# Writing out 39 expert slots on every engine, and a new way of numbering and adding their results

## What is computed

```
x = x + attention(layernorm(x), context)
bids = sigmoid(h @ conf_w.T + conf_b) * wealth        # h = layernorm(x), 8 experts
top_bids, selected = top_k(bids, 2)
weights = softmax(top_bids)
expert_e(h) = (silu(h @ gate_e.T) * (h @ up_e.T)) @ down_e.T     # 128 -> 512 -> 128
x = x + weights[0] * expert_first(h) + weights[1] * expert_second(h)
```

## Time and profile before

| what | us |
|---|---|
| median of 3 runs | 534.74 (534.35 to 538.36) |
| the profiled execution | 535.53 |
| its span in the trace | 533.8 |
| PE busy | 475.3 |
| DVE busy | 352.8 |
| ACT busy | 313.2 |
| POOL busy | 168.9 |

### The profile page before, as it was taken

The page is one execution under the profiler, slowest core; times in us unless marked ns, Lnnn a source line. Parts: engine busy times, 40 slices in busy tenths (PEclk is TensorE's granted clock), DMA queues, the critical chain, the costliest instruction groups (busy, mean ns, idle before and its releaser), DMA issues. The chain is left out here.

```text
span 533.8 us, 11413 instructions
## 1 busy us (share of the span) xinstructions
PE 475.3 (89%) x4013; PEld 334.3 (63%) x4014; DVE 352.8 (66%) x646; ACT 313.2 (59%) x625; POOL 168.9 (32%) x301
## 2 busy tenths in 40 slices
PE   7789999999999999999999987979987888878840
PEld 7455555555555565555555534978887887878840
DVE  7788797888887987987889823686233332323317
ACT  2248787787777877777878784302454554445500
POOL 8141412312412312324111001023555556455420
PEclk9659999999999999999999998896999999899995
DMA  7503143243342343331222000800211111111126
GB/s 191 140 21 91 46 101 100 76 114 99 91 124 78 89 119 85 80 91 47 61 56 62 18 1 6 233 1 5 41 37 41 34 39 39 34 39 34 34 74 183
DMA packets 32257, 38.14 MB, mean 71 GB/s; under 512 B 5604, under 2 KB 20580, under 8 KB 32212
## 3 DMA queue, kind: packets, MB, share of 16 engines
q1 hardware_dynamic: 27252, 30.79, 21.5%
q0 software_dynamic: 2560, 5.25, 3.8%
q10 hardware_dynamic: 2400, 1.51, 1.0%
HBM read 16.58 MB, written 4.72 MB: 40 GB/s over the span
## 5 line engine op out<-in xcount | busy, mean ns | idle before, releaser
L469 DVE TENSOR_REDUCE max_part<-max_ps 128x2 f32<-128x1024 f32 (+1 forms) x192 | 226.0, 1221 | 38.3 <-PE max_ps L567 29.9
L428 ACT ACTIVATE probs<-ring_ps 128x512 f32<-128x512 f32 x384 | 198.4, 604 | 51.0 <-PE ring_ps L590 47.8
L590 PE MATMUL ring_ps<-blocks,keys 64*128 64x512 f32 x384 | 151.7, 474 | 2.1 <-ACT probs L428 1.6
L600 PE MATMUL pv_ps<-probs,value_cols 128*32 128x256 f32 x1536 | 103.4, 388 | 0.0
L567 PE MATMUL max_ps<-keys,blocks 64*128 64x512 f32 x256 | 84.2, 448 | 3.6 <-DMA blocks<-masked 2.5
L590 PEld LDWEIGHTS ring_ps<-blocks,keys 64*128 64x128 f32 x384 | 65.7, 187 | 31.6 <-ACT probs L428 25.2
L1012 DVE COPY xT<-t_ps 128x128 f32<-128x128 f32 x40 | 11.7, 292 | 86.2 <-remote 44.4
L600 PEld LDWEIGHTS pv_ps<-probs,value_cols 128*32 128x32 f32 x1536 | 40.3, 109 | 40.2 <-issue 18.3
L1111 PE MATMUL gate_ps<-xT,staged 128*128 128x128 f32 x320 | 43.8, 280 | 21.0 <-DVE xT L1012 21.0
L341 POOL CAST maxes<-rowmax 128x8 fp32r<-128x8 f32 x32 | 6.3, 198 | 169.5 <-DVE rowmax L476 169.5
L873 POOL DMA_INDIRECT pick_outs<-y_out,target x40 | 39.5, 988 | 53.4 <-DVE y_out L1028 49.2
(11 more groups left out here) (149 smaller groups left out, 491.4 us busy)
## 6 DMA issues: line engine op xcount, KB each, us to landing
keys<-parts SPq DMA_DIRECT2D x96, 96.0 KB
blocks<-masked SPq DMA_DIRECT2D x93, 64.0 KB
ctx_v_sb<-ctx_v_dram SPq DMA_DIRECT2D x8, 256.0 KB, 2.9
gate<-gateT_dram SPq DMA_DIRECT2D x8, 256.0 KB, 2.8
up<-upT_dram SPq DMA_DIRECT2D x8, 256.0 KB, 2.9
y_in<-pick_outs SPq DMA_DIRECT2D x8, 256.0 KB, 4.7
raw<-ctx_kT_dram SPq DMA_DIRECT2D x7, 256.0 KB, 2.7
h_rows<-h SPq DMA_DIRECT2D x4, 256.0 KB, 5.3
```

The source lines that it names most:

```text
L428: act.activation(probs[par][:, k, PAIR * a:PAIR * (a + 1)], bank("exp", s * XUNITS + u)[:].rearrange("p (g n) -> p g n", n=N), ACT.Exp).th ...
L469: vec.reduce_max(out, bank, axis=AX.X).then_inc(max_done, 1)
L590: pe.matmul(ps[:], keys[rows, t, k * P:(k + 1) * P], blocks[rows, t], start=True, stop=True)\
L600: mm = pe.matmul(pv_ps[ROWS * g:ROWS * (g + 1), 0:N], value_cols[:, t, k, g, :], probs[q % 2][:, k, g, :], start=(k == 0), stop=(k == KT - 1))
```

## The change

Four edits, all in `experts`:

1. `slots` has no loop any more: PE, DVE and ACT write out every slot, and all semaphore values are constants. The last slot is the 39th (`SLOTS`), where the kernel before ran 40. POOL loads and stores one slot less too.
2. Picks are numbered by partition first: pick k of partition p, tile t is k * 2048 + 16 * p + t + 1. `h_rows` and `pick_outs` have their rows in this order, so that what a partition reads or writes in a chunk of four tiles is one run of 2 KB in DRAM rather than four of 512 bytes.
3. The eight loads of results are split: SP issues the four of the first picks, ACT the four of the second picks, each with its own semaphore (`load_picks`).
4. The second picks' results are multiplied by their weights on ACT (16 instructions, 128 x 128, in place in `y_in`). DVE adds weight times result of the first pick as before (16 instructions), and then one 128 x 512 addition for each chunk adds ACT's products.

```diff
-        def slots(engine, step, last):
-
-            for j in range(8):
+        def slots(step, last):
+
+            for j in range(last):
                 step(*divmod(j, 4))
-            with engine.Fori(2, SLOTS_PAD // 4 - 1) as i:
-                for r in range(4):
-                    step(i, r)
-            for r in range(last - (SLOTS_PAD - 4)):
-                step(SLOTS_PAD // 4 - 1, r)
...
+        def load_picks(engine, k):
+
+            rows = outs_dram[k * TILES * P:(k + 1) * TILES * P, :].rearrange("(p t) c -> p t c", t=TILES)
+            for r in range(4):
+                engine.wait_ge(y_stored[r], 16 * len(range(r, SLOTS, 4)))
+            for c in range(CHUNKS):
+                engine.dma_start(y_in[:, k, c * CHUNK:(c + 1) * CHUNK, :], rows[:, c * CHUNK:(c + 1) * CHUNK, :])\
+                      .then_inc(y_loaded[2 * c + k], 16)
...
-                sp.dma_start(h_dram[k * 4 * P:(k + 1) * 4 * P, :].rearrange("(t p) c -> p t c", p=P),
+                sp.dma_start(h_dram.rearrange("(p t) c -> p t c", t=TILES)[:, k * 4:(k + 1) * 4, :],
                              h[:, k * 4:(k + 1) * 4, :]).then_inc(h_stored, 16)
-            for r in range(4):
-                sp.wait_ge(y_stored[r], 16 * (SLOTS_PAD // 4))
-            for c in range(CHUNKS):
-                for k in range(2):
-                    n = TILES // CHUNKS
-                    first_row = (k * TILES + c * n) * P
-                    sp.dma_start(y_in[:, k, c * n:(c + 1) * n, :],
-                                 outs_dram[first_row:first_row + n * P, :].rearrange("(t p) c -> p t c", p=P))\
-                      .then_inc(y_loaded[c], 16)
+            load_picks(sp, 0)
...
-            iota(pick_id[:], [[P, 2 * TILES]], 1, 1)
+            iota(pick_id[:], [[TILES * P, 2], [1, TILES]], 1, TILES)
...
-            for j in range(SLOTS_PAD + 2):
-                if j + 3 < SLOTS_PAD:
+            for j in range(SLOTS + 2):
+                if j + 3 < SLOTS:
...
-            slots(act, step, SLOTS_PAD)
...
+            slots(step, SLOTS)
+            def weigh_second(c):
+                act.wait_ge(y_loaded[2 * c + 1], 16)
+                for t in range(c * CHUNK, (c + 1) * CHUNK):
+                    act.activation(y_in[:, 1, t, :], y_in[:, 1, t, :], ACT.Copy, scale=weight[:, 1, t, :]).then_inc(second_weighted, 1)
...
+            load_picks(act, 1)
             for c in range(CHUNKS):
...
+                weigh_second(c)
+                if c:
+                    store_rows(c - 1)
+            store_rows(CHUNKS - 1)
...
-            slots(vec, step, SLOTS_PAD + 1)
-            for t in range(TILES):
-                if t % (TILES // CHUNKS) == 0:
-                    vec.wait_ge(y_loaded[t // (TILES // CHUNKS)], 32)
-                if t == 0:
-                    vec.wait_ge(weights_done, 1)
-                for k in range(2):
-                    if k:
-                        vec.wait_ge(summed, 2 * t + 1)
-                    vec.scalar_tensor_tensor(m.x[:, t, :], y_in[:, k, t, :], weight[:, k, t, :], m.x[:, t, :],
-                                             ALU.mult, ALU.add).then_inc(summed, 1)
+            slots(step, SLOTS + 1)
+            vec.wait_ge(weights_done, 1)
+            for c in range(CHUNKS):
+                vec.wait_ge(y_loaded[2 * c], 16)
+                for t in range(c * CHUNK, (c + 1) * CHUNK):
+                    vec.scalar_tensor_tensor(m.x[:, t, :], y_in[:, 0, t, :], weight[:, 0, t, :], m.x[:, t, :],
+                                             ALU.mult, ALU.add).then_inc(first_added, 1)
+                vec.wait_ge(first_added, (c + 1) * CHUNK)
+                vec.wait_ge(second_weighted, (c + 1) * CHUNK)
+                rows = m.x[:, c * CHUNK:(c + 1) * CHUNK, :]
+                vec.tensor_tensor(rows, rows, y_in[:, 1, c * CHUNK:(c + 1) * CHUNK, :], ALU.add).then_inc(summed, 1)
```

More of the change, by code:

```diff
@@ L701 @@
 CHUNKS = 4
+CHUNK = TILES // CHUNKS
 def experts(nc, m, d, out):
@@ L730, in experts @@
         picks_found, sources_ready = sem("picks_found"), sem("sources_ready")
-        y_loaded = [sem(f"y_loaded{i}") for i in range(CHUNKS)]
+        y_loaded = [sem(f"y_loaded{i}") for i in range(2 * CHUNKS)]
         x_loaded = [sem(f"x_loaded{i}") for i in range(4)]
@@ L793, in experts @@
         block = ctx.enter_context(nc.Block())
-        def slots(engine, step, last):
-            for j in range(8):
+        def slots(step, last):
+            for j in range(last):
                 step(*divmod(j, 4))
-            with engine.Fori(2, SLOTS_PAD // 4 - 1) as i:
-                for r in range(4):
-                    step(i, r)
-            for r in range(last - (SLOTS_PAD - 4)):
-                step(SLOTS_PAD // 4 - 1, r)
         def exists(i, r, shift):
-            return not isinstance(i, int) or 0 <= 4 * i + r + shift < SLOTS_PAD
+            return 0 <= 4 * i + r + shift < SLOTS
         def hot_slot(engine, k):
@@ L915, in _, with store_rows @@
             stage(0, 0)
-            slots(act, step, SLOTS_PAD)
-            n = TILES // CHUNKS
+            slots(step, SLOTS)
[3 more added lines that the diff above has]
+                    act.activation(y_in[:, 1, t, :], y_in[:, 1, t, :], ACT.Copy, scale=weight[:, 1, t, :]).then_inc(second_weighted, 1)
+            def store_rows(c):
+                act.wait_ge(summed, c + 1)
+                act.dma_start(out.rearrange("b (t p) c -> p (b t) c", p=P)[:, c * CHUNK:(c + 1) * CHUNK, :],
+                              m.x[:, c * CHUNK:(c + 1) * CHUNK, :]).then_inc(stored, 16)
+            load_picks(act, 1)
             for c in range(CHUNKS):
-                act.wait_ge(summed, 2 * n * (c + 1))
-                act.dma_start(out.rearrange("b (t p) c -> p (b t) c", p=P)[:, c * n:(c + 1) * n, :],
-                              m.x[:, c * n:(c + 1) * n, :]).then_inc(stored, 16)
+                weigh_second(c)
+                if c:
+                    store_rows(c - 1)
+            store_rows(CHUNKS - 1)
             act.wait_ge(stored, 16 * CHUNKS)
@@ L1025, in step @@
                     vec.wait_ge(y_filled, j)
-                    if not isinstance(i, int) or j >= 5:
+                    if j >= 5:
                         vec.wait_ge(y_stored[(r - 1) % 4], (i if r >= 1 else i - 1) * 16)
@@ L1136, in _ @@
             transpose_x(0, 0, 0)
-            slots(pe, step, SLOTS_PAD + 1)
+            slots(step, SLOTS + 1)
 def kernel(x, ctx_2048, L0_xattn_w_qkv, L0_xattn_w_proj, L0_xattn_b_proj, L0_ffn_conf_w, L0_ffn_conf_b,
```

3 lines of the change are left out of this document (2 added, 1 removed).

## The result

The changed kernel takes **533.26 us** (median of 16 runs), the kernel before 537.93 (16 runs) beside it: a ratio of 0.9911 [0.9886, 0.9935], 4.8 us less (3.5 to 6.1 by the interval). The forecast was 7.2 less, a ratio of 0.9865. It also leaned on the 534.74 of three runs; sixteen give 3.2 us more, and the absolute forecast is low by that as well. The profiled execution took 532.04 with a span of 530.3; before it was 535.53 and 533.8.

The account below looks back on a forecast made before the run. The prediction took the chain of waits as the bound, with a serial end where every microsecond saved counts. One slot less, adding up and loads gave -3.5 - 3.3 - 0.4 = -7.2 us, from 534.74 to 527.5 us, range 523 to 533.

Parts of the forecast that it names:

- Writing out: 0: Slots: writing them out instead of looping changes nothing, 0 us, between -3 and +4.
- The fetch rival: Slots: fetching the written-out code costs what the loop saved, giving 534.7 us; chance 8%.
- The rival that the loop makes the stalls: Slots: stalls belong to the loop, so nine of twelve go, 18.5 us, giving 509; chance 8%.
- the rule of the Trainium skill: Slot loop: taken branches can force instruction fetches, giving seven fetch stalls to regain; the sum had no term for it.
- The slower rhythm: Slots: written-out slots fall into the slower rhythm of pairs, +3.5 us, giving 531; chance 20%.
- One slot less: -3.5: Slots: dropping one saves a slow slot, as the quick stretch begins earlier; -3.5 us, between -2.8 and -3.5.
- Adding up: -3.3: Final additions: 7.17 us against 10.49 with ACT weighing second picks; -3.3 us, between -2 and -4.
- its deadline for the last chunk: Loads of results: the last chunk must be there 5.3 us after the first, at about 525.5.
- bound by something new: Adding up: ACT's products or the loads' second half limit it at 2.6 us a chunk, giving 530.8; chance 6%.
- Loads: -0.4: Loads of results: the second load comes from ACT at once, 0.4 us earlier; between -1 and +2.3.
- The numbering's bad end: Last scatter: rows at least 8 KB apart could double its 2.26 us, making the end 2.3 us later.
- The sum: Whole kernel: slot, adding up and loads, -3.5 - 3.3 - 0.4 = -7.2 us, giving 527.5 us.

Follow-up runs that it names:

- e9: Kernel before with all 40 slots written out and nothing else, on a chip that stalls: 538.74 us, ratio 1.0 to the kernel before.
- e2: Kernel before with all 40 slots written out and nothing else, on a chip without stalls: 512.49 us, ratio 0.9994 to the kernel before.
- e5: Kernel before with only the numbering by partition, on a chip that stalls: 537.16 us against 538.09, ratio 0.9997.
- e8: Changed kernel once more, unaltered, on a chip that stalls: 532.29 us against 538.81 for the kernel before, ratio 0.9886.
- e1: Kernel before with one slot less, loop kept, on a chip without stalls: 509.23 us against 512.70, ratio 0.9949.
- e12: Changed kernel with DVE and ACT waiting for all eight loads before they add: 510.83 us against 513.12 for the kernel before, ratio 0.9971.
- e3: Kernel before with only ACT's weighing of second picks and the wide additions, all loads on SP: 511.31 us, ratio 0.9964.
- e4: Changed kernel with all eight loads of results issued by SP: 508.69 us, ratio 0.991 to the kernel before.
- e15: Changed kernel with odd slots' gathers replaced by SP's loads of consecutive rows, on a chip that stalls: 516.09 us (one run), kernel before 541.46.
- e10: Changed kernel with more buffers, work around PE one slot further ahead, gathers five ahead: 524.37 us, ratio 0.9743 to the kernel before.
- e6: Changed kernel with POOL's gathers replaced by SP's loads of consecutive rows: 504.31 us (one run), kernel before 538.09.
- e7: Changed kernel with POOL's scatters replaced by SP's stores of consecutive rows: 506.12 us (one run), kernel before 538.09.

## Why the prediction was right or wrong

**Right in direction and in what the engines do, wrong in size:** 4.8 us of 7.2.

*Writing out: 0.* Right, and now shown by itself on both kinds of chip: 0.9994 and 1.000. The fetch rival is refuted: 33 instruction packets against 28, and PE's share unchanged. The rival that the loop makes the stalls is refuted by e9, which has none left of the loop and stalls as much. So is the rule of the Trainium skill ("Runtime: NRT & Kernel Launch", Instruction fetch mechanics) as a source of gain here: the loop's seven turns on each engine gave back nothing that 12 runs can tell (1.5 us either way in e2). The slower rhythm came true in form, pairs instead of triples, but not in price: 3.56 us a slot against 3.54.

*One slot less: -3.5.* Too large in this pair of profiles, where the term is -2.78, and open in general. The prediction argued that one gather less lets the quick stretch begin a slot earlier. In the two profiles of the comparison it didn't: the last stall ends with `xT` of slot 35 in both, with four slots behind it before and three now, so a quick slot went. But where the last stall ends depends on the rhythm. With 40 slots it ends with slot 35 before, with slot 36 in e9 and with slot 37 in e5; with 39 slots it ends with slot 35 in both profiles of the changed kernel. Between e9 and e8, both written out and both in pairs, the quick stretch did begin a slot earlier, and 3.81 us went. From slot 0 to the last `xT` the three profiles with 40 slots take 133.35, 134.83 and 134.23 us, the two with 39 slots 130.87 and 131.02: 2.3 to 4.0 us for the slot. The argument is not refuted; what it left out is that the loop's rhythm can end a stall early, as it did in the profile that it was read from. e1 decides nothing here, since nothing stalled on its chip.

*Adding up: -3.3.* **This step failed, together with the next.** The term is -2.67, and -2.3 in e8. The engines' side was nearly right: 7.17 us forecast, 7.35 in e12, where all data are there. What failed is the statement on the waits, "So the first chunk may wait 0.1 us. Later ones don't." DVE waits for ACT 0.40 us in the first chunk and 0.29 in the third, and 0.42 and 0.64 in e8. The landing signals in the trace show why. A chunk has two loads, and the later one of each chunk is in 3.98, 5.45, 7.79 and 8.76 us after the first issue. DVE's first addition starts at 3.84. In the first chunk ACT's load comes 0.25 us after SP's, and its products take 1.28 us where DVE's four additions take 1.14. At 1.77 us a chunk the third chunk's turn comes at 3.84 + 2 x 1.77 = 7.38 us, and the second picks that ACT must multiply for it land at 7.79. In the eleven profiles with two queues that load lands 7.65 to 8.24 us after the first issue.

The loads as a whole did not become slower. Before, the four chunks were in after 3.66, 6.09, 8.01 and 9.57 us, while DVE used up a chunk in 2.6 us, so they kept ahead of it. The prediction's "the same transfers come no later than now" came true in this profile for all but the first chunk (in e8 the third is later too, 8.24), and its deadline for the last chunk was met too: 5.3 us after the first addition allowed, 4.92 measured. It checked the last chunk only, and the third is the one that is late. With one queue the same wait is longer: 8.42 us of adding up in e3, 8.50 in e4. The rival "bound by something new" named the right limiter, the second half of the loads; it put the chunk at 2.6 us, and it is some 2.

*Loads: -0.4.* Wrong sign: +0.15 and +0.23. The prediction took the second load's issue for the limit. In the two profiles with 2 KB runs and one queue the first pair is in after 4.17 and 4.34 us, with two queues after 3.81 to 4.08. So the second queue did bring what it was to bring, some 0.3 us, but the new numbering had taken some 0.5, which the prediction had left to the range with the other sign. The Trainium skill says that a second issuing engine brings no bandwidth ("DMA: Bandwidth & Descriptors", Issuing engines are not separate DMA queues: what SP and ACT issue goes through the same engines, and only the time to issue is saved). The traces agree as far as they go: the last of the eight loads is issued 2.06 us sooner than in e4 (1.36 us after the first instead of 3.42) and lands 0.84 sooner (8.76 against 9.60). The numbering's bad end did not come (last scatter 2.24 us; e5).

*The sum.* By the profiled executions -2.78 - 2.67 + 0.15 + 0.03 = -5.3, of which the chance delay before slot 0 (+1.5) and the slots (+0.3) leave -3.5; in e8, on another chip and without the delay, the span is 4.9 us shorter than in the profile before. By the ratios: -4.8, -6.1, and -4.6 for e4's form. What is missing against -7.2 is 0.6 to 1.0 of the adding up and 0.6 of the loads, which every profile of the changed kernel shows, and in this pair 1.0 over all the slots (130.87 - 133.35 = -2.48 against -3.5), which e9 and e8 don't show (-3.81).

## What to carry to other kernels

Price a removed iteration by where the slow stretch ends in the trace, and give both prices if that place moves from one rhythm to the other. Before a consumer behind loads is made faster, read from the trace when each load lands, and compare every one with the new, shorter schedule, not only the first and the last; a wait that is hidden now is the next bound. And where a stall's releaser has no name, look at what all the other engines do as it ends, and take their work away one kind at a time.

## What the runs showed of the hardware

**The stalls need POOL's indirect transfers of both kinds, and they depend on the chip.** In the stall of the earlier trace rows PE's matmuls are recorded on schedule, but the engines that wait for them start late and nearly together. More rows of that timeline of the kernel before:

```profile
408.27 0.97 POOL L867 DMA_INDIRECT x_in<-h_rows,source  x1 [0.30 <-issue]
...
409.56 0.99 POOL L873 DMA_INDIRECT pick_outs<-y_out,target  x1 [0.31 <-issue]
...
410.54 0.60 ACT L911 ACTIVATE silu<-gate_ps 128x512 f32<-128x512 f32 x1 [1.85 <-PE gate_ps L1111]
...
412.81 0.63 ACT L899 ACTIVATE staged<-gate 128x512 f32 x1 [1.67 <-remote]
412.96 0.68 DVE L1022 TENSOR_TENSOR hiddenT<-up_ps,silu 128x512 f32<-128x512 f32 x1
```

The gate product ended at 409.31, and its signal came at 410.52, while POOL's run of indirect transfers still went on. The up product ended at 410.20, the transpose at 410.31, the down product at 411.2; their signals came at 412.70 to 412.82, up to 2.5 us late and within 0.12 us, 0.9 us after the run had ended (411.82). In e15 it is 0.8 to 1.0 us after the end of the run, in e10 1.2, with a hold of 4.4 us after a longer run. POOL pauses because its next scatter needs the held signal, so the order of cause isn't proven by one trace. That the holds need POOL's transfers of both kinds is shown by e6 and e7, that they shorten with a shorter run by e15, if by one profile.

PE's signals are not the only ones affected. Each of POOL's transfers raises its semaphore 16 times as it lands. In e9, on a chip that stalls, the trace has 2 to 5 of the 16 signals for 46 of the 56 transfers whose successor starts within 0.9 us of POOL's end with them, and all 16 for 21 of the 24 others. In e2, the same kernel on a chip that doesn't stall, it has all 16 for each of the 80. The trace can't say whether the missing signals came together or only went unrecorded.

Yet the same run is harmless on another chip. POOL's first scatter and gather pairs, in the changed kernel on a chip that stalls:

```profile
383.34 1.01 POOL L871 DMA_INDIRECT pick_outs<-y_out,target  x1 [2.83 <-DVE y_out L1037]
384.66 0.98 POOL L865 DMA_INDIRECT x_in<-h_rows,source  x1 [0.30 <-PE t_ps L1116]
386.13 1.00 POOL L871 DMA_INDIRECT pick_outs<-y_out,target  x1 [0.50 <-issue]
387.43 0.97 POOL L865 DMA_INDIRECT x_in<-h_rows,source  x1 [0.30 <-issue]
390.46 1.00 POOL L871 DMA_INDIRECT pick_outs<-y_out,target  x1 [2.06 <-DVE y_out L1037]
```

and in e2's written-out kernel on a chip that doesn't:

```profile
384.88 1.01 POOL L868 DMA_INDIRECT pick_outs<-y_out,target  x1 [2.83 <-DVE y_out L1023]
386.20 0.97 POOL L862 DMA_INDIRECT x_in<-h_rows,source  x1 [0.30 <-PE t_ps L1102]
387.67 0.99 POOL L868 DMA_INDIRECT pick_outs<-y_out,target  x1 [0.50 <-DVE y_out L1023]
388.97 0.97 POOL L862 DMA_INDIRECT x_in<-h_rows,source  x1 [0.30 <-PE t_ps L1102]
390.46 1.00 POOL L868 DMA_INDIRECT pick_outs<-y_out,target  x1 [0.52 <-DVE y_out L1023]
```

Four instructions at nearly the same distances; then one chip goes on after 0.52 us and the other after 2.06. It is worth 25 us in the whole kernel (513 against 538). What holds the signals, and why only on some chips, stays open, and so does whether POOL's pacing would help on a chip that stalls.
